# A gated recurrent layer on one core: rotation products in one run by head pair, eight product buffers, preparation and edges rearranged

## The reference

```python
xn = layernorm(x)
proj = xn @ in_proj_w.T            # z, xin, B, C, dt, theta, lam
Bm, Cm = rms(B) * w + B_bias, rms(C) * w + C_bias     # per head: 32 heads, N = 64
tc = cumsum(theta, axis=1)
Bm, Cm = rope(Bm, tc), rope(Cm, tc)   # v1*cos - v2*sin, v1*sin + v2*cos
# scan over tokens, per head, state h of 64 x 64
h = alpha * h + gamma * outer(x_t, B_t) + beta * outer(x_prev, B_prev)
y = h @ C_t + D * x_t
s = rms(y * silu(z), norm_w) @ out_proj_w.T
g = silu(fake_fp8(xn) @ fake_fp8(ffn_w).T + ffn_b)
out = x + s * g
```

## Time and profile before

| | |
|---|---|
| runs | 1225.22, 1233.62, 1225.27 us; median 1225.27 |
| the profiled execution | 1226.61 us, its span 1224.8 us |
| barrier between the parts | about 141 us into the span |
| first rotation product of the units | 149.13 us |
| yT of the first unit | 178.38 us |
| last product run ends, yT starts | 1199.33 us |
| busy | PE 92%, DVE 94%, ACT 67%, POOL 63% |

### The profile page before, as it was taken

How to read it: one execution, slowest core, us unless ns; L and a number is a source line. 1 busy time by engine, 2 the same in 40 slices (tenths; PEclk the granted TensorE clock), 3 DMA queues, 4 the chain that set the end, 5 groups by cost and what they waited for, 6 DMA issues and landing times.

```text
span 1224.8 us, 30431 instructions
## 1 busy us (share of the span) xinstructions
PE 1128.6 (92%) x11442; PEld 818.2 (67%) x11442; DVE 1156.3 (94%) x1795; ACT 819.0 (67%) x1270; POOL 771.2 (63%) x594
## 2 busy tenths in 40 slices
PE   3876579999999999999999999999999999999996
PEld 3652256777776776777677767777777767777675
DVE  7899489999999999999999999999999999999994
ACT  4677356676767676667676676677676766777663
POOL 5002046776777667777766677776776687667774
PEclk9976589999999999999999999999999999999999
DMA  8633646444654455545644465446445555444540
GB/s 191 202 103 94 145 91 144 110 94 110 148 123 105 105 124 120 122 107 117 141 108 103 94 155 123 98 112 137 112 109 112 124 128 123 103 89 104 122 100 15
DMA packets 91888, 142.94 MB, mean 117 GB/s; under 512 B 19326, under 2 KB 38591, under 8 KB 91327
## 3 DMA queue, kind: packets, MB, share of 16 engines
q1 hardware_dynamic: 91743, 141.00, 49.6%
HBM read 58.68 MB, written 13.37 MB: 59 GB/s over the span
## 4 chain that ended last, share of the span: by engine, by line
PE 58%; DVE 11%; issue 9%; POOL 6%; ACT 1%; DMA 1%; SPq 1%; DVEq 0%; POOLq 0%; ACTq 0%
PE y L1210 9%; PE r L1196 8%; PE s L1113 7%; PE o L1128 6%; PE r L1087 5%; PE r L1093 5%; PE y L1204 4%; PE y L1220 4%; PE r L1082 3%; PE r L1168 3%; PE d L1102 3%; POOL rot L1477 3%; DVE bw L1284 2%; DVE hs L1333 2%; DVE M L1292 2%
## 5 line engine op out<-in xcount | busy, mean ns | idle before, releaser
L1477 POOL TENSOR_TENSOR rot<-part 128x512 f32<-128x512 f32 x256 | 383.3, 1497 | 303.5 <-DVE part L1274 303.5
L1274 DVE SCALAR_TENSOR_TENSOR part<-bcs,k_prmT,k_trig 128x512 f32<-128x512 f32 x512 | 535.1, 1095 | 18.7 <-SPq L1030 15.1
L1408 ACT ACTIVATE E<-d 128x512 f32<-128x512 f32 x256 | 152.8, 597 | 182.9 <-PE d L1102 182.6
L1486 POOL TENSOR_TENSOR ce<-rot,eb 128x512 f32<-128x512 f32 x128 | 186.7, 1478 | 0.4 <-POOLq L1521 0.3
L1292 DVE TENSOR_TENSOR M<-s,E 128x512 f32<-128x512 f32 x256 | 164.0, 679 | 2.8 <-PE s L1113 1.8
L1528 POOL TENSOR_TENSOR sqa<-sqa,sq 128x512 f32<-128x512 f32 x112 | 142.6, 1274 | 31.7 <-ACT sq L1418 23.7
L1087 PE MATMUL r<-k_w_zx,xns 128*128 128x256 f32 x512 | 136.9, 391 | 19.1 <-DMA xns<-xn_t 13.5
L1113 PE MATMUL s<-rot 64*128 64x128 f32 x2048 | 149.7, 286 | 1.8 <-POOL rot L1477 1.8
L1413 ACT COPY xk<-r 128x512 f32<-128x512 f32 x128 | 75.3, 588 | 112.1 <-PE r L1087 112.1
L1113 PEld LDWEIGHTS s<-rot 64*128 64x128 f32 x2048 | 125.3, 188 | 37.3 <-issue 36.8
L1210 PE MATMUL y<-M,xk 128*64 128x128 f32 x2048 | 140.1, 279 | 0.0
(11 more groups left out here) (254 smaller groups left out, 1695.9 us busy)
## 6 DMA issues: line engine op xcount, KB each, us to landing
k_trig<-k_tri SPq DMA_DIRECT2D x512, 128.0 KB, 2.4
eb<-ecum_rows SPq DMA_DIRECT2D x128, 256.0 KB, 4.7
bcs<-bc_t SPq DMA_DIRECT2D x16, 256.0 KB, 4.2
bcs<-bc_t SPq DMA_DIRECT2D x32, 128.0 KB, 3.9
a_big<-in_L_attn_u SPq DMA_DIRECT2D x4, 512.0 KB, 6.2
xn_t<-a_xnT SPq DMA_DIRECT2D x1, 2048.0 KB, 11.1
tc_t<-a_tcT SPq DMA_DIRECT2D x1, 2048.0 KB, 15.5
bc_t<-a_tmp SPq DMA_DIRECT2D x1, 2048.0 KB, 8.5
```

The lines of the kernel that those rows point to most:

```text
L1274: nc.vector.scalar_tensor_tensor(out=part[:, 2 * p + f, :], in0=bcs[:, (t + q // NQ) % 2, 2 * w + f, :], scalar=col, in1=trig[:, p, 1 - f, ...
L1408: nc.scalar.activation(E[:, h % 2, :], Dp[:], ACT.Exp).then_inc(e_ready, 1)
L1477: nc.gpsimd.tensor_tensor(rot[:, q % 2, p, w, :], part[:, 2 * p, :], part[:, 2 * p + 1, :], ALU.add).then_inc(rot_ready, 1)
L1486: nc.gpsimd.tensor_tensor(ce[:, p, :], rot[:, q % 2, p, 1, :], eb[:, p, :], ALU.mult).then_inc(ce_ready, 1)
```

## The change

In the units: the eight products stand in one run behind both halves of xc, by pair (p = 0: B, C; p = 1: B, C), with eight buffers, so no product waits for a sum of its own group. Both sums of pair 0 wait for all four products of that pair; those of pair 1 wait for six and eight products. TensorE's scores take B and C of pair 0 after two sums, and the transposes are split, the second behind the first scores; `project` is no longer split. The norm's refinement moves from GpSimd to VectorE (three instructions between products and behind yT), and the finish of a stretch moves into the sums of q = 2 and q = 3. In the preparation: the first load of B, C and tokens is issued before the barrier (their buffers are now shared with `a_big`), `dup` is set first behind the barrier, the two subtractions go to VectorE, the gate's bias product runs up to three tiles ahead in four banks.

The diff, cut to what the steps speak of:

```diff
 # prepare, SyncE: before the barrier
+            sp.wait_ge(stored[0], 16)
+            sp.dma_start(K["xns"][:, 0, :], xn_d[0]).then_inc(xn_loaded, 16)
+            sp.wait_ge(stored[2], 16)
+            sp.wait_ge(pr_done, 1)
+            sp.wait_ge(bcT_t, 8)
+            load_bc(sp, K, bc_d, 0, bc_loaded)
...
 # prepare, GpSimd
-            for i in range(2):
-                pool.wait_ge(log_cut, i + 1)
-                nc.gpsimd.tensor_tensor(s[2]..., s[2]..., cum3[:, :, H * i:H * i + H], ALU.subtract).then_inc(log_left, 1)
+            pool.wait_ge(kk_done, 2)
             pool.wait_ge(dec_done, 1)
...
 # prepare, TensorE: gate bias, up to three tiles ahead
+            gate_bias(0)
+            gate_bias(1)
             for t in range(NS):
-                b = ps[2 + t % 2]
-                if t >= 2:
-                    pe.wait_ge(g_done, t - 1)
-                nc.tensor.matmul(b[:], ones[0:1, :], bias4[:], start=True, stop=False, skip_group_check=True)
+                b = ps[2 + t % 4]
...
 # prepare, VectorE, behind quantise of tile t
+                if t in (1, 3):
+                    i = t // 2
+                    dve.wait_ge(log_cut, i + 1)
+                    lg = s[2].rearrange("p (c h) -> p c h", h=H)
+                    nc.vector.tensor_tensor(lg, lg, cum3[:, :, H * i:H * i + H], ALU.subtract).then_inc(log_left, 1)
...
 # units
-        part = sb("part", [P, 4, ST])
+        part = sb("part", [P, 8, ST])
 # SyncE
-                    sp.wait_ge(part_ready, at(T8, t, 8 * (q - 1) + 6 + 2 * p))
+                    sp.wait_ge(part_ready, at(T8, t, 8 * (q - 1) + 4 + 4 * p))
-            load_bc(0)
-            sp.dma_start(xns[:, 0, :], xn_d[0]).then_inc(xn_loaded, 16)
+            for p in range(2):
+                sp.sem_inc(dup[p], DUP)
...
-            for p in range(2):
-                sp.sem_inc(dup[p], DUP)
 # TensorE
-                pe.wait_ge(rot_ready, at(T4, t, 4 * q + 3 + p))
+                pe.wait_ge(rot_ready, at(T4, t, 4 * q + 2 + 2 * p))
...
-                    if t + q > 0 and q != 1:
-                        project(t, q - 1, (0, 1))
...
-                        project(t, q - 1, (2, 3) if q != 1 else range(CS))
+                        project(t, q - 1, range(CS))
...
+                    transposed(0)
                     exponents(t, q + 1, 0)
                     scores(t, q + 1, 0)
+                    transposed(1)
                     exponents(t, q + 1, 1)
 # VectorE
-                    if live(t, q + 1):
-                        rotation(t, q + 1, 0, 0, 0)
                     if live(t, q + 2):
                         angles(t, q + 2)
                     for c in range(CS):
                         state(t, q, c)
-                    if live(t, q + 1):
-                        rotation(t, q + 1, 0, 0, 1)
-                        x_scaled(t, q + 1, tn, 0)
                     scores(t, q, 2)
                     scores(t, q, 3)
                     if q == 0 and t > 0:
                         norm_start(t - 1)
                     if live(t, q + 1):
+                        x_scaled(t, q + 1, tn, 0)
                         x_scaled(t, q + 1, tn, 1)
-                    if live(t, q + 1):
-                        for p, w in ((1, 0), (0, 1), (1, 1)):
+                        for p, w in ((0, 0), (0, 1), (1, 0), (1, 1)):
                             rotation(t, q + 1, p, w, 0)
                             rotation(t, q + 1, p, w, 1)
-                            if q == 0 and t > 0 and (p, w) == (1, 0):
+                            if q == 0 and t > 0 and p == 0 and w == 1:
                                 norm_seeded(t - 1)
+                            if q == 0 and t > 0 and p == 1:
+                                norm_refined(t - 1, w)
...
 # GpSimd
-                w, p = k // 2, k % 2
-                pool.wait_ge(part_ready, at(T8, t, 8 * q + 2 * k + 2))
+                p, w = k // 2, k % 2
+                pool.wait_ge(part_ready, at(T8, t, 8 * q + (2 * k + 2 if p else 4)))
...
                         for k in range(4):
                             sums(t, q + 1, k)
+                            if k == 0 and q == 2 and t > 0:
+                                gated_out(t - 1)
+                            if k == 0 and q == 3 and t > 0:
+                                finished(t - 1)
```

More of the change, by code:

```diff
@@ L1374, in _ @@
             norm_seeded(NS - 1)
+            for i in range(3):
+                norm_refined(NS - 1, i)
             dve.wait_ge(acc_done, at(1, NS, 0))
@@ L1504, in finished @@
                 nc.gpsimd.tensor_tensor(so[:], so[:], gate[:], ALU.mult).then_inc(gated, 1)
+            def finished(t):
                 pool.wait_ge(gated, t + 1)
```

147 lines of the change are left out of this document (81 added, 66 removed).

## The result

The changed kernel took 1273.87 us (median of 4 runs, 1273.23 to 1276.06), the kernel before beside it 1229.22 (1225.22 to 1233.62): ratio 1.037, 95% interval 1.032 to 1.042. It is 3.7% slower. The forecast was 1272. The profiled execution took 1273.23, its span 1271.3.

The account below looks back on a forecast made before the run. VectorE was taken to bound the kernel. 1226.6 + 57.7 (units) - 11.3 (edges) = 1273.0 us profiled, the median 1.3 below: 1272, 3.8% slower; range 1236 to 1286, with the first rival 1224 to 1288.

Parts of the forecast that it names:

- the three held products: In VectorE's run of eight, products 6, 7 and 8 each held by a GpSimd sum, taking 1.69 instead of 0.67 us.
- the waits for the copies: VectorE's xc halves wait for ScalarE's copies of x by token: 0.04 + 0.27 us idle in an odd unit.
- The special units: Units at q = 0 to 3 with extra work: 2.1 us a stretch, 15 us over seven stretches, bounds 0 to 25.
- the two terms of the edges: Gains before the first product: 4.0 us in the preparation (bounds 2 and 6.5), 7.3 behind the barrier (6 and 7.5).
- The run of eight: VectorE's eight products in one run, five at 0.67 and three held at 1.69: 8.42 us, against 8.26 before.
- Rival 2: Only two sums fall into the run, so a unit has 1.02 us less: total 1209, faster; chance 0.06.
- Rival 3: A held product waits out the whole sum, 1.93 us instead of 1.69: 45 us more, total 1317; chance 0.02.
- What the singles covered: Waits on VectorE formerly hidden by single products, at ang and xc: +0.72 us in an odd unit, yT distance 17.02.
- Rival 1: Nothing waits: ang and xc come in time, only VectorE's work counts, units +12.4 us, total 1226, no change; chance 0.14.
- The units' sum: The 62 yT distances: regular units 1063.6 us plus 15 for special units make 1078.6, +57.7 on 1020.95.
- Unseen: Chance 0.02 for anything not foreseen, such as a slower TensorE clock while it waits more; no time given.
- The edges: Preparation and start of the second part, before the first product: a gain, -11.3 us together.

Follow-up runs that it names:

- e9: The changed kernel with each GpSimd sum on 256 of 512 columns, the other half set to 1 once (rotated values wrong there): 1178.82 us, ratio 0.961.
- e5: The changed kernel with the first product of the run moved between the two xc halves: 1258.93 us, ratio 1.026 to the kernel before.
- e2: The changed kernel with each sum let go by its own products, pair 0's by two and four instead of four and four: 1294.71 us, ratio 1.057.
- e1: The kernel before's units with only the changed kernel's preparation and start of the second part: 1216.04 us, ratio 0.991 to the kernel before.
- e8: The kernel before's units with the changed kernel's edges, its norm on VectorE and its finish at q = 2 and 3: 1208.74 us, ratio 0.986.
- e11: e4 with TensorE's order of before as well (projection split, both groups of transposes together): 1213.39 us, ratio 0.991 to the kernel before.
- e4: e3 with each sum let go by its own two products: 1233.19 us, ratio 1.004 to the kernel before.
- e3: The changed kernel with VectorE's order of before (products 1 and 2 single, M between the xc), sums still tied to four products: 1255.34 us, ratio 1.024.
- e7: The changed kernel with products set apart, each pair followed by VectorE work reading PSUM, and each sum let go by its own pair: 1183.65 us, ratio 0.966.
- e12: e7 with TensorE's order of before (both transposes together, projection split): 1199.51 us, ratio 0.979 to the kernel before.
- e6: The changed kernel with four extra matmuls in unit q = 0 of each stretch, to keep TensorE busy: 1277.62 us, ratio 1.039 to the kernel before.

## Why the prediction was right

It was right in total (1272 for 1273.87) and in its mechanism: the three held products and the waits for the copies. The special units, the two terms of the edges and TensorE's clock were each off, and that they cancel is luck.

1. **The run of eight**: 8.42 predicted, 8.35 measured, by the pattern named: five distances of 0.66, three of 1.68. Rival 2 (two sums only) is refuted by the three distances. Rival 3 asked for 1.93 a held product; the Trainium skill (SBUF — State Buffer, Who interferes with whom) has the later instruction blocked until the first has finished. e9 shows the exclusion, and shows too that the hold is a sum's length less 0.25 at both widths, so the sentence is true to within that quarter.
2. **What the singles covered**: predicted 0.24 at `ang` and 0.31 at `xc`; measured by the starts 0.22 and 0.33 in the unit from 655.08, 0.28 and 0.12 in the next, where the states took the rest. The second `xc` was put at 8.00 after yT, and came at 8.02 and 8.08. Units 17.02 and 17.29 for 16.98 and 17.22. e5 confirms the cause from the other side: one product in the gap, 0.26 less. Rival 1 (nothing waits, 1226) is refuted by both rows.
3. **The units' sum**: 1078.6 predicted, 1078.5 measured. This agrees better than its parts do, and that is luck. Regular units came 0.055 lower than predicted in the mean, 3.4 us over 62. What lies above them is 18.3 (1078.5 - 31 x 34.20), not 15, but 6 of it are the half clock of point 4; the special units themselves cost 12.3. At the run of q = 0 1.25 a stretch, for 1.4; at q = 1 0.5, for 0.2; at q = 2 and 3 nothing, for 0.54. There the third sum did end 1.2 us after yT and the second transposes did wait for it, as predicted, but the angles started 1.98 after yT instead of 1.93 and not 0.27 later: TensorE's stand of 1.2 to 1.5 us ahead of the angles took the delay in. That no fourth product was held there hangs on the late start of pair 0's sums; e2 shows what it costs otherwise (1.02).
4. **Unseen**: four stretches of TensorE at half clock, 3.4 us long and worth 1.5 us each, 6 us in all. The prediction had given 0.02 to all that it had not seen, a slower clock of a TensorE that waits more among it. In the kernel before the clock is full from the first yT to the last run; in the changed one it fell after four of seven stands of 1.69 to 1.91 us. The sum had no term for it; without the four stretches the units would have come to 1072.5.
5. **The edges**: -11.3 predicted; the first product came 11.2 earlier and e1 gained 10 in the median. The two terms were each off and cancelled: the preparation gave 5.8 (4.0 predicted), as the quantising has neither the held instructions nor the waits of the earlier trace rows, and the start 5.5 (7.3 predicted): idle before the first product fell from 15.12 to 9.67.

Where the loss lies, in one chain of the 62 distances: before 1020.95; norm and finish (e8) -7.0; eight buffers, pair order, own sums (e11) +2.8; TensorE's order (e4) +15.7; pair 0's sums held to four products (e3) +27.1; one run (the change) +18.9, of which 6 are the half clock. The prediction put the units at +57.7 by three collisions, uncovered waits and special units; that holds for the whole, but the chain shows a division that it did not make: TensorE's new order, for which it had no term, costs 0.25 a unit where VectorE keeps singles, while with e7's order of VectorE it gains 16 us (e12). Steps of such a chain depend on their order; only the ends don't.

## What to carry to other kernels

Count which operations of two engines that read SBUF stand side by side, not how many buffers lie between them: here each GpSimd sum that fell into a run of VectorE's products, which read two inputs from SBUF, held it for nearly the sum's own length. Put the producer's pairs ahead of work that reads PSUM (e7), so that the consumer runs beside that. Before joining work into one run, look at what each of its pieces stood in front of: a single instruction that seems misplaced may be the cover of a wait.

## What the hardware showed that I had not expected

- The hold is the other instruction's length less 0.25 us: 1.02 for 1.27, 0.49 for 0.73 (e9).
- TensorE's clock fell to half for 3.4 us inside full work, in four of seven like places with stands of 1.69 to 1.91 us, at 1.5 us each. After the stands of at most 1.56 us there in all other units of the changed kernel it never fell, but in e5 and e6 it fell in the first unit after a stand of 1.47.
- The preparation, unchanged between the profiles of kernels that share it, takes 166 to 176 us to the first yT, and that goes with how long TensorE is at half clock in it: 61 us in the profiles with a first yT at 166.2 to 167.6, 79 in those at 168.0 to 169.7, 85 to 89 in those at 173 to 176. A gain of 6 us in the units can drown in that (e6); the distances inside the profile show it.
